# A Swin-style attention and MLP block on one core: the projection's bias carried in idle rows of its fifth product, the probability transposes fed with 128 columns, and the pieces of a step placed in another order

## What is computed

```python
xl = _ln(transpose(x, (0, 2, 3, 1)), norm1_w, norm1_b)
xl = roll(xl, (-3, -3), axis=(1, 2))
xw = windows(xl, 7)                                   # (16*64, 49, 192)
q, k, v = (xw @ qkv_w.T + qkv_b) in 6 heads of 32
attn = softmax(q @ k.T * 32**-0.5)
out = (attn @ v) @ proj_w.T + proj_b
xl = roll(unwindow(out), (3, 3), axis=(1, 2))
xl = _ln(xl, norm2_w, norm2_b)
h = gelu(xl @ fc1_w.T + fc1_b) @ fc2_w.T + fc2_b
return transpose(h, (0, 3, 1, 2)) + shortcut
```

## Time and profile before

| | |
|---|---|
| median of 3 runs | 3363.76 us (3362.97 to 3364.15) |
| the profiled execution | 3362.43 us |
| its span in the profile | 3360.3 us |
| TensorE (PE) busy | 3294.9 us, 98% |
| weight loads (PEld) busy | 3205.5 us, 95% |
| VectorE (DVE) | 2742.4 us, 82% |
| ScalarE (ACT) | 2513.4 us, 75% |
| GpSimd (POOL) | 980.2 us, 29% |

### The profile page before, as it was taken

How to read it: one execution, slowest core, us unless ns; L and a number is a source line. 1 busy time by engine, 2 the same in 40 slices (tenths; PEclk the granted TensorE clock), 3 DMA queues, 4 the chain that set the end, 5 groups by cost and what they waited for, 6 DMA issues and landing times.

```text
span 3360.3 us, 79720 instructions
## 1 busy us (share of the span) xinstructions
PE 3294.9 (98%) x29100; PEld 3205.5 (95%) x29100; DVE 2742.4 (82%) x7857; ACT 2513.4 (75%) x4990; POOL 980.2 (29%) x1288
## 2 busy tenths in 40 slices
PE   3999999999999999999999999999999999999998
PEld 3999999999999999999999999999999999999998
DVE  4888888888888888888888888888888888888886
ACT  1777777777777777777777777777777777777776
POOL 0223223322322332232233233223223322322332
PEclk9999999999999999999999999999999999999999
DMA  2000100110010011001001100100110010011000
GB/s 51 16 23 23 30 23 23 26 27 23 23 30 23 23 27 27 23 23 29 24 23 27 27 23 23 30 23 23 27 27 23 23 30 23 23 27 27 23 16 19
DMA packets 128409, 84.22 MB, mean 25 GB/s; under 512 B 70705, under 2 KB 127794, under 8 KB 128050
## 3 DMA queue, kind: packets, MB, share of 16 engines
q1 hardware_dynamic: 128050, 79.32, 9.3%
HBM read 40.71 MB, written 38.54 MB: 24 GB/s over the span
## 4 chain that ended last, share of the span: by engine, by line
PE 97%; DVE 1%; SPq 1%; ACT 0%; DMA 0%; issue 0%; POOL 0%; POOLq 0%; DVEq 0%; ACTq 0%
PE psum L496 8%; PE psum L280 7%; PE psum L284 6%; PE psum L282 6%; PE psum L281 6%; PE psum L283 6%; PE psum L475 5%; PE psum L438 5%; PE psum L466 4%; PE psum L481 4%; PE psum L455 4%; PE psum L467 4%; PE psum L456 4%; PE psum L457 4%; PE psum L416 3%; PE psum L291 3%
## 5 line engine op out<-in xcount | busy, mean ns | idle before, releaser
L1010 POOL TENSOR_TENSOR pr<-pr,rc 98x294 f32<-98x294 f32 x512 | 423.0, 826 | 1848.8 <-DVE rc L872 1848.8
L806 DVE BATCH_NORM_STATS2 st<-psum 98x6 f32<-98x192 f32 x1024 | 354.5, 357 | 289.2 <-PE psum L416 217.9
L628 ACT ACTIVATE hh<-psum,b 128x392 fp32r<-128x392 f32 x768 | 453.3, 590 | 92.0 <-PE psum L284 89.2
L817 DVE TENSOR_SCALAR xn<-psum,mv,rs 98x192 f32<-98x192 f32 x1024 | 436.8, 469 | 18.9 <-POOL rs L998 4.3
L631 ACT ACTIVATE hf<-psum,b 128x392 f32<-128x392 f32 x768 | 442.1, 594 | 0.0
L881 DVE COPY vbd<-psum 49x192 f32<-49x192 f32 x1024 | 357.8, 349 | 37.3 <-PE psum L294 22.3
L836 DVE TENSOR_TENSOR hl<-hf,hh 128x392 fp32r<-128x392 f32 x640 | 347.1, 559 | 9.4 <-ACT hf L631 9.4
L466 PE MATMUL psum<-hl,w2h 128*128 128x392 f32 x768 | 285.6, 372 | 0.3 <-DVE hl L836 0.3
L606 ACT ACTIVATE x_h<-psum 128x392 fp32r<-128x392 f32 x256 | 126.7, 495 | 210.2 <-PE psum L438 210.2
L859 DVE TENSOR_REDUCE mx<-psum 98x6 f32<-98x294 f32 x512 | 235.1, 460 | 52.6 <-PE psum L476 45.5
L455 PE MATMUL psum<-hh,w2h 128*128 128x392 f32 x768 | 275.3, 358 | 0.0
(11 more groups left out here) (133 smaller groups left out, 10233.0 us busy)
## 6 DMA issues: line engine op xcount, KB each, us to landing
xt<-in_x SPq DMA_DIRECT2D x112, 194.5 KB, 2.5
out<-xt SPq DMA_DIRECT2D x112, 194.5 KB, 1.9
xt<-in_x SPq DMA_DIRECT2D x112, 97.2 KB, 2.6
out<-xt SPq DMA_DIRECT2D x112, 97.2 KB, 2.2
xt<-in_x SPq DMA_DIRECT2D x128, 1.5 KB, 2.2
xt<-in_x SPq DMA_DIRECT2D x128, 0.8 KB, 2.0
out<-xt SPq DMA_DIRECT2D x128, 1.5 KB, 1.8
out<-xt SPq DMA_DIRECT2D x128, 0.8 KB, 1.7
```

Source lines behind the costliest of these rows:

```text
L628: nc.scalar.activation(hh[:, m % HB, :], bank("fc1", m)[:, 0:T], ACT.Gelu, bias=b1[:, m:m + 1]).then_inc(s_hh, 1)
L817: nc.vector.tensor_scalar(xn[ln][:, j, :], ln_chunk(("ln1", "ln2")[ln], j), mv[ln][:, j, 0:1], rs[ln][:, j:j + 1], ALU.subtract, ALU.mult) ...
L1010: nc.gpsimd.tensor_tensor(probs(j), probs(j), each, ALU.mult).then_inc(s_prob, 1)
```

## The change

1. The bias of the projection moves into the fifth product. The last weight tile, wrl, of the projection is filled in its rows 0 to 63 only by the weights; row 64 now holds the bias's high part, row 96 its low part, the other rows are zero. A fifth version of the attention output, `o_b`, has the high part of the last 64 channels in rows 0 to 63 and ones in rows 64 to 127, and is loaded for the fifth product. ScalarE writes rows 0 to 63 of it with one more 64x392 instruction per unit. The sixth product is gone. Before, rows 64 to 127 of the fifth product multiplied the activations' low parts by the low parts of the weights; these terms now fall away.
2. A transpose of the probabilities loads 128 columns of `pr` in place of 113 (the added columns belong to the next block or are zero) and writes 128 partitions; the copy after it reads the same 113.
3. `BANK_USES` and the order of the pieces of a step on all four engines are new. `values` 0 and 1, `scores` 0, `fc1` 0 and 1 and `qkv` 2 come one step earlier, at the end of a step; `scaled_probs` on GpSimd and the exponentials on ScalarE move with them in their lists.

The diff, cut to its core (the lists of pieces are shown by the rows behind it):

```diff
-BANK_USES = [("qkv", 2, 3, 2), ("fc1", 0, 5, 4), ("vt", 0, 0, 2), ("fc1", 1, 4, 4), ("fc1", 2, 1, 4),
...
+BANK_USES = [("fc1", 2, 1, 4), ("s", 1, 2, 2), ("fc2", 0, 3, 4), ("fc2", 1, 5, 4), ("s", 2, 4, 2),
...
+             ("pt", 2, 3, 2), ("ln1", 1, 2, 0), ("pt", 3, 0, 2), ("x2", 1, 7, 3), ("qkv", 2, 5, 1),
...
-        def five_tokens(ps, w, act, stop):
+        def five_tokens(ps, w, act, last=None):
...
-            return nc.tensor.matmul(ps, xrr, wrl[:, 0:C], start=False, stop=stop)
+            return nc.tensor.matmul(ps, xrr if last is None else last, wrl[:, 0:C], start=False, stop=True)
...
-                five_tokens(ps, wp, [p[:, TP * j:TP * j + TP] for p in o], False)
-
-                last = nc.tensor.matmul(ps, ones[:, :], bp[:, :], start=False, stop=True)
+                last = five_tokens(ps, wp, [p[:, TP * j:TP * j + TP] for p in o], o_b[:, TP * j:TP * j + TP])
...
-                    last = nc.tensor.transpose(bank("pt", j)[0:KP, TP * p:TP * p + TP],
-                                               pr[:, j, 2 * WP * p:2 * WP * p + KP], ident[0:TP, 0:TP])
+                    last = nc.tensor.transpose(bank("pt", j)[:, TP * p:TP * p + TP],
+                                               pr[:, j, 2 * WP * p:2 * WP * p + 2 * WP], ident[0:TP, 0:TP])
...
                 if name == "o":
-
+                    if g == 1:
+                        biased(o_b[0:m, :], src, bq[0:m, g:g + 1], s_hi[name])
                     biased(HI_LO[name][dst][0:m], src, bq[0:m, g:g + 1], s_hi[name])
...
+            nc.vector.tensor_copy(wp[3][64:65, :], pb_hi[:, :].bitcast(F32))
+            nc.vector.tensor_tensor(wp[3][96:97, :], pb[:, :], pb_hi[:, :].bitcast(F32), ALU.subtract)
```

More of the change, by code:

```diff
@@ L566, in step @@
                 if u[4] is not None:
-                    fc2_lo(u[4], 3)
+                    fc2_hi(u[4], 3)
                     fc2_hi(u[4], 4)
+                if u[2] is not None:
+                    probs_t(u[2], 0)
+                if u[4] is not None:
+                    fc2_hi(u[4], 5)
                 if u[2] is not None:
@@ L571, in step @@
                 if u[4] is not None:
-                    fc2_hi(u[4], 5)
+                    fc2_lo(u[4], 3)
                     fc2_lo(u[4], 4)
-                if u[2] is not None:
-                    probs_t(u[2], 2)
-                if u[4] is not None:
                     fc2_lo(u[4], 5)
+                if u[1] is not None:
+                    qkv(u[1], 3)
+                if u[3] is not None:
+                    x2_channels(u[3], 0)
                 if u[0] is not None:
@@ L580, in step @@
                     to_tokens(u[0], k, it, 1)
+                if u[2] is not None:
+                    probs_t(u[2], 2)
+                if u[0] is not None:
                     to_tokens(u[0], k, it, 2)
@@ L595, in step @@
                     weighted(u[2], 3)
+                if u[1] is not None:
+                    values(u[1], 0)
+                    scores(u[1], 0)
+                if u[3] is not None:
+                    fc1(u[3], 0)
+                if u[1] is not None:
+                    values(u[1], 1)
+                if u[3] is not None:
+                    fc1(u[3], 1)
             steps(step)
@@ L1033, in step @@
                     rstd(0, u[0])
+                if u[1] is not None:
+                    scaled_probs(u[1], 0)
+                if u[2] is not None:
+                    rstd(1, u[2])
+                if u[1] is not None:
+                    scaled_probs(u[1], 1)
+                if u[3] is not None:
+                    hidden_lo_last(u[3])
+                if u[1] is not None:
+                    scaled_probs(u[1], 2)
+                    scaled_probs(u[1], 3)
             steps(step)
```

223 lines of the change are left out of this document (98 added, 125 removed), and 11 rows, old and new, of the table BANK_USES.

## The result

The change takes **3285.28 us** (median of 4 runs, 3283.83 to 3286.31) beside 3363.36 us for the kernel before on the same chip: the ratio is 0.9767, 95% interval 0.975 to 0.9784. The sign was right, the size was not. The profiled execution took 3283.83 us, with a span of 3282.1 us.

A forecast was written before the change was run, and what follows sets the result against it. TensorE's back-to-back work was taken as the bound. 0.356 + 0.12 - 0.03 = 0.446 us a unit, times 128 units 57.1 us, gave 3307 us for the median, range 3295 to 3326 us.

The forecast's parts named there:

- What bounds the kernel: Whole kernel: TensorE's own work laid end to end, 25.56 us a step, with no wait for other engines.
- Sixth product: Projection: each of a unit's four pairs loses one matmul of 0.089 us, saving 0.356 us a unit.
- Transposes with 128 columns: Probability transposes: loading 128 columns instead of 113 saves 0.03 us a group, four groups, 0.12 us a unit.
- Rival 1: Probability transposes: 128 columns load no faster (3322 us) or slower (3337 us, or 3335 by the skill page); 12% together.
- New order: TensorE's order: more wide products stand behind transposes or scores, costing a net 0.03 us a unit.
- `weighted`: Its entry and exit on TensorE with new neighbours: no difference, 0.10 us a unit either way, 13 us.
- Rival 2: TensorE's neighbours: `weighted` and each wide product behind scores lose 0.10 us; 0.24 us a unit more, 3338 us; 7%.
- No added wait: `probs_t` 2 waits for `finish_main` with a margin of 0.2 to 0.9 us, so added wait is 0.
- Rival 3: GpSimd's scaling and root delay `finish_main`, so PE waits at `probs_t` 2: 0.45 us a step slower, 3452 us; 6%.
- 0.18 among its like: TensorE: a wide product behind other wide products takes 0.18 us, taken the same before and after.

The follow-up runs named there:

- the small program: Computes nothing of the reference: phases of 48 products of 128x392, tile starts varied, alone or beside other engines; three versions, 175.5 to 180.0 ns a product.
- later start: The change plus one fill of 700 numbers on VectorE before the first step, no address moved: 3286.31 us, ratio 0.9771.
- the sweep: The small program with TensorE alone, loaded tiles 1024 bytes apart, moving start varied over 1024 bytes: 177.4, 180.0, 175.5, 177.8 ns at 0, 64, 128, 192.

## Why the prediction was right or wrong

- **What bounds the kernel: right.** PE's own work laid end to end, no waits of PE for others after the change either, and the whole gain in the step.
- **Sixth product, 0.356 us a unit: right.** 512 products fewer, 0.088 us each in the rows. With the bias alone, the step's 0.465 us is 0.356 and the wide products' 0.108.
- **Transposes with 128 columns, 0.12: right.** Forecast were 248 ns and 0.46 us, measured 247 and 0.46; by the ends of all groups the inner pitch fell from 99.2 to 84.4 ns, eight times 14.8 = 0.118 us. The edit alone gave 18.9 us, 0.151 us a step, 0.118 of it here and 0.018 in slightly cheaper wide products. Rival 1 fell: its two forms had the transposes at 0.10 or 0.115. The page "TensorE: Matmul & The Clock Gate" of the Trainium skill, in its section on the weight-path modes, keeps the fast load from FP32; here a float32 tile of 128 columns goes 15 ns faster than one of 113, so the time does not simply grow with the loaded columns, whatever the cause.
- **New order, -0.03: right as a price of neighbours, not as the effect of the order.** In the kernel with the order alone the step fell by 0.023 us where it was to rise by 0.03. The wide products give 27 x 0.6 + 26 x 1.3 - 14 x 0.6 = 0.042 of that, which leaves a cost of 0.02 for the neighbours. So the order, too, moved the pitch that the sum held constant.
- **`weighted`, no difference, 0.10 either way: right.** 0.09 in and 0.17 out, for 0.10 and 0.19. Rival 2 fell with it, and wide behind scores cost 0.21 us, not 0.28.
- **No added wait: right.** Rival 3 did not occur; `finish_main` waits for PE.
- **The step that failed:** in the part on the new order a wide product costs "0.18 among its like", and this 0.18 was taken as a constant of the shape. So the sum has no term for a wide product behind another; it put their change at nothing, without a reason. It was 0.1797 and became 0.1766 for `fc1`, 0.1796 and 0.1779 for `fc2`, 0.1908 and 0.1893 for `qkv`. 67 such pitches a unit make 0.149 us, 19 us of the 22 by which the forecast missed. With the activations back at their old addresses the same program takes 3304.6 us, and its wide pitches keep only 0.016 of the 0.149 us. The diff shows tiles taken out and put in; the prediction priced their fills, and not that everything behind them moves.
- The remaining 0.015 us a step, 2 us, lies among some twenty entry and exit costs that were rounded. The largest of them fits its size: by the averages a narrow product behind `weighted` pays 0.178 us over its usual pitch, where the wide one paid 0.195.

The same page of the Trainium skill, in its section "Wait — 56ns, not 53.3ns?", gives for the gap between neighbouring matmuls N / 2.4 GHz and about 2.5 ns more, which would be an estimate of 165.8 ns for 392 columns. None of the runs here agrees, in which each product also loads its own tile: the lowest is 175.5 ns, and the place of the tiles moves it by up to 4.5.

**What stays open.** The rule by which addresses set the pitch in the whole kernel. The distance modulo 256 has the wrong sign for the step from the old addresses to the new, and kernels with equal distances for `fc2` differ by up to 1.5 ns in its pitch. Why 256 bytes is the period in the small program is open too. One later start left the change's pattern as it was; in the small programs 32 and 96 bytes had two values each, so how a pattern is entered may count there. The small program excludes the other engines at start 0, and the PSUM bank, for its own stream; the neighbouring products, whose tiles stand at other distances, remain. Some ten placements were tried; the best one was not searched for.

## What to carry to other kernels

In a kernel that is bound by back-to-back matmuls, an edit that allocates or frees a tile also moves every tile allocated behind it in SBUF, and here that was worth 19 of 78 us. So measure such an edit once more with a pad that restores the old addresses before you credit it, and give a range for a constant that is multiplied by 67 a step: 2 ns in it are 17 us. When the kernel is done, a few pads of 32 or 64 bytes are cheap to try: the kernel before would have had 12 us for one.

## What the runs showed of the hardware

- A float32r product of 128 loaded and 392 moving columns has no single pitch at the full clock of 2.4 GHz: 175.5 to 180.0 ns in the small programs. With the moving tile 0, 64, 128 and 192 bytes from the loaded ones, modulo 256, it is 177.4, 180.0, 175.5 and 177.8, repeated to 0.5 ns; at odd multiples of 32 one start can have two values, 2 ns apart. It comes in short repeating patterns, at distance 128 for instance 178, 173, 176 ns.
- The first 7 to 13 pitches of the three small programs were 326 to 328 ns, which is 392 columns at 1.2 GHz. The profile prints a granted clock of 1.00 for that stretch too, but that is no measurement: the traces hold no clock record from before the pitch had fallen (the first begins 11.8 us into the sweep's span, and one trace has none).
- VectorE, ScalarE and GpSimd, reading and writing SBUF and reading PSUM beside it, changed the pitch by at most 0.1 ns at an unmoved start.
- Loading 128 columns of a float32 tile is faster than loading 113: 84 against 99 ns of pitch with 98 columns moving, and also faster than the scores, which load 98, at 87.
